# Pair 0's first element with a plain second product, block sums behind the last split, and x split first at the turn to stage two

## The reference

```python
def _L0(x, adj, S, W1, W2, W3):          # called with S = adj, so the weighting is adj * adj
    def _slconv(x, adj, S, W):
        return einsum('nm,bmh->bnh', adj * S, einsum('bnf,fh->bnh', x, W))
    h = relu(_slconv(x, adj, S, W1))     # 128 -> 256 features
    h = relu(_slconv(h, adj, S, W2))     # 256 -> 512
    return _slconv(h, adj, S, W3)        # 512 -> 128
def _L1(x, adj, Wg0, bg0, Wg1, bg1, Wih, Whh, bih, bhh):
    h = relu(einsum('ts,bsh->bth', adj, x @ Wg0 + bg0))
    h = relu(einsum('ts,bsh->bth', adj, h @ Wg1 + bg1))
    ...                                  # LSTMs over windows of p = 1..4 nodes
    return h
x = _layernorm(x + _L0(x, adj, adj, W1, W2, W3))
x = _layernorm(x + _L1(x, adj, ...))
```

## Time and profile before

| | |
|---|---|
| median of 3 runs | 1001.5 us (1000.24 to 1001.92) |
| the profiled execution | 1000.72 us |
| its span in the trace | 998.5 us |
| PE busy in the span | 970.3 us, 97% |
| DVE, ACT, POOL busy | 660.7, 434.8, 58.4 us |
| mean granted clock of PE | 0.99 |

### The profile page before, as it was taken

How to read it: one execution, slowest core, us unless ns; L and a number is a source line. 1 busy time by engine, 2 the same in 40 slices (tenths; PEclk the granted TensorE clock), 3 DMA queues, 4 the chain that set the end, 5 groups by cost and what they waited for, 6 DMA issues and landing times.

```text
span 998.5 us, 14421 instructions
## 1 busy us (share of the span) xinstructions
PE 970.3 (97%) x5267; PEld 846.1 (85%) x5267; DVE 660.7 (66%) x1447; ACT 434.8 (44%) x796; POOL 58.4 (6%) x46
## 2 busy tenths in 40 slices
PE   9789999999999999999989999999999999999994
PEld 7568898888988899888978889898988989898894
DVE  7865456654465554755396556877677786777987
ACT  6533323244133330343334444545454454554765
POOL 2600010002000020000000000101010010100000
PEclk9899999999999999999999999999999999999998
DMA  8000010200102001012700000000000000000001
GB/s 301 0 1 1 1 43 1 85 1 1 43 0 84 0 3 40 21 64 96 273 1 1 1 1 1 1 1 22 2 1 22 0 21 0 21 2 21 1 1 63
DMA packets 11287, 30.99 MB, mean 31 GB/s; under 512 B 1121, under 2 KB 2401, under 8 KB 11233
## 3 DMA queue, kind: packets, MB, share of 16 engines
q1 hardware_dynamic: 11232, 30.30, 8.3%
HBM read 22.95 MB, written 7.34 MB: 30 GB/s over the span
## 4 chain that ended last, share of the span: by engine, by line
PE 87%; DVE 8%; ACT 2%; issue 2%; DMA 1%; SPq 0%; DVEq 0%; ACTq 0%
PE ps L1201 23%; PE ps L866 20%; PE ps L842 10%; PE ps L843 10%; PE ps L844 10%; PE ps L1042 8%; PE ps L1254 2%; PE ps L1274 2%; DVE adj L1677 1%; DVE tile_sum L2096 1%; PE ps L1034 1%; DVE sx L1677 1%; PE ps L1316 1%; DVE stats L1694 1%; DMA xb<-in_x 1%
## 5 line engine op out<-in xcount | busy, mean ns | idle before, releaser
L866 PE MATMUL ps<-adj,t 128*128 128x512 f32 x528 | 124.9, 390 | 3.3 <-DVE y_raw L1868 1.5
L866 PEld LDWEIGHTS ps<-adj,t 128*128 128x128 f32 x528 | 98.1, 188 | 24.1 <-DVE y_raw L1868 2.0
L1042 PE MATMUL ps<-s,adj 128*128 128x256 f32 x768 | 94.0, 284 | 0.0
L866 PE MATMUL ps<-sx,t 128*128 128x512 f32 x396 | 92.1, 390 | 1.2 <-DVE sx L1677 0.8
L1042 PEld LDWEIGHTS ps<-s,adj 128*128 128x128 f32 x768 | 92.6, 192 | 0.0
L866 PEld LDWEIGHTS ps<-sx,t 128*128 128x128 f32 x396 | 74.2, 188 | 17.4 <-DVE sx L1677 1.2
L842 PE MATMUL ps<-adj,node 128*128 128x512 f32 x216 | 85.0, 394 | 2.5 <-DVE adj L1677 2.4
L844 PE MATMUL ps<-adj,node 128*128 128x512 f32 x216 | 84.8, 392 | 0.0
L843 PE MATMUL ps<-adj,node 128*128 128x512 f32 x216 | 84.6, 392 | 0.0
L1615 ACT ACTIVATE gates_x<-ps,lb 128x258 f32<-128x258 f32 (+1 forms) x156 | 66.5, 508 | 40.3 <-PE ps L1201 40.1
L1615 ACT ACTIVATE gates<-ps,lb 128x512 f32<-128x512 f32 (+2 forms) x117 | 66.7, 647 | 37.9 <-PE ps L1201 28.7
(11 more groups left out here) (244 smaller groups left out, 1806.8 us busy)
## 6 DMA issues: line engine op xcount, KB each, us to landing
xb<-in_x SPq DMA_DIRECT2D x7, 1024.0 KB, 4.8
sx_raw<-in_adj_t SPq DMA_DIRECT2D x8, 512.0 KB, 8.2
adj_raw<-in_adj_t SPq DMA_DIRECT2D x8, 512.0 KB, 7.2
out<-xb SPq DMA_DIRECT2D x7, 512.0 KB, 2.6
xn<-xb SPq DMA_DIRECT2D x3, 1024.0 KB, 4.0
xb<-xn SPq DMA_DIRECT2D x6, 512.0 KB, 6.6
xb<-in_x SPq DMA_DIRECT2D x2, 512.0 KB, 5.3
lw_raw<-in_wih_t SPq DMA_DIRECT2D x1, 1024.0 KB, 11.4
```

The lines of the kernel that those rows point to most:

```text
L866: last = pe.matmul(dst, t7[:, B_BLOCK[v], a, tile], A_BLOCK[v](b, t), start=start and t == 0 and (a, b) == (HI, HI), stop=t == QUARTER - 1 ...
L1042: last = pe.matmul(dst, adj[:, a, m, nt:nt + P], s3[:, b, m, :, :].rearrange("p j c -> p (j c)"), start=(m == 0 and t == 0 and (a, b) == ( ...
```

## The change

Three edits.

1. The second adjacency product of element 0 of pair 0 is done plainly: eight blocks, 96 matmuls, on the parts of the adjacency matrix itself and of the relu of the W1 product, whose high and low parts are now taken straight from PSUM ("0 h1 0" to "0 h1 3"; the low part in two instructions each). The T sums, the block sums' waits and the additions on DVE go away for this element.
2. The block sums on POOL begin when the low part of the last tile ("adj7") is there. A21 - A11 moves from DVE to POOL (four instructions more there, 16 in all). The splits of W2 and W3, of S1, S2, S3 and S4 move to later places: W2, W3 and S1 behind "0 h1 3", S2 behind the four C blocks, S3 and S4 among the h2 blocks.
3. In the last pair ACT takes "n x" and the high parts of tiles 0 and 1 of the new adjacency matrix before "from a11".

```diff
+        PLAIN = ["0 C11", "0 C12", "0 C21", "0 C22"]
-        MM_FIRST = ["x0 0", "x0 1", "x1 0", "x1 1"] + w1_names(0, 0, 4) + seven(0, FIRST_ORDER) + MM_TAIL
+        MM_FIRST = ["x0 0", "x0 1", "x1 0", "x1 1"] + w1_names(0, 0, 4) + PLAIN + MM_TAIL
+        X_H1 = ["x C12", "x C22", "0 h1 0", "0 h1 1", "x C11", "x C21", "0 h1 2", "0 h1 3", "w2 w3", "S1"] + PLAIN
-        HI_FIRST = (PRE + ["x C12", "x C22", "S1", "0 raw 0", "0 raw 1", "0 B11", "0 T1", "x C11", "x C21", "0 raw 2",
-                           "0 raw 3", "0 B21", "0 T2", "S2", "0 p1", "0 B22", "S4", "0 T3", "S3", "0 T4"]
-                    + hi_second(0, *C_FIRST) + HI_TAIL)
+        HI_FIRST = (PRE + X_H1 + ["S2"] + h2_names(0, 0, 0, K3) + ["S3"] + h2_names(0, 1, 0, 2) + ["S4"]
+                    + h2_names(0, 1, 2, K3) + HI_TAIL)
-        HI_LAST = HI_START + hi_second(0, *C_ORDER) + HI_ONE + FROM_A11 + ["n x"]
+        HI_LAST = HI_START + hi_second(0, *C_ORDER) + HI_ONE + ["n x"] + FROM_A11
-        LO_FIRST = (PRE + ["S3 sum", "x C12", "x C22", "0 T1 sum", "0 B11", "S1", "0 T2 sum", "0 T1", "x C11", "x C21",
-                           "0 T4 sum", "0 B21", "0 T2", "S2", "0 q", "0 T3 sum", "0 B22", "S4", "0 T3", "S3", "0 T4",
-                           "0 C11", "0 r"] + lo_second(0, *LO_C_FIRST) + LO_TAIL)
+        LO_FIRST = (PRE + X_H1 + ["S2"] + h2_names(0, 0, 0, K3) + ["S3"] + h2_names(0, 1, 0, 2) + ["0 s3t 0", "S4"]
+                    + h2_names(0, 1, 2, K3) + LO_TAIL)
...
+            pool.wait_ge(a_lo, prepared("adj7"))
             for t in range(QUARTER):
-                pool.wait_ge(*((sq_act, 5), (sq_done, 5), (sq_act, 6), (sq_done, 6))[t])
-                if t == 0:
-                    pool.wait_ge(sq_done, 1)
                 nc.gpsimd.tensor_tensor(sx_raw[:, S1, LO, t, :], a21(t), a22(t), ALU.add).then_inc(block_sum, 1)
...
+            for t in range(QUARTER):
+                nc.gpsimd.tensor_tensor(s3_diff[:, t, :], a21(t), a11(t), ALU.subtract).then_inc(block_sum, 1)
...
+                def plain_part(k, rows, half):
+                    of, dst = ((B11, T3), (B21, B22))[rows][k], bank("0 " + (("a", "e"), ("b", "c"))[k][half])
+                    for t in range(QUARTER):
+                        lo_done(f"0 h1 {2 * rows + t // 2}")
+                        last = product(dst, lambda i: t7[:, of, i, t * P:(t + 1) * P],
+                                       lambda i: adj[:, i, rows * QUARTER + t, half * BANK:(half + 1) * BANK],
+                                       (rows, t) == (0, 0), (rows, t) == (1, QUARTER - 1))
+                    return last
+                def plain_adjacency():
+                    for k in range(K2):
+                        if k == 1:
+                            lo_done("x C11", "x C21")
+                        for half in range(HALVES):
+                            plain_part(k, 0, half)
+                    for half in range(HALVES):
+                        for k in range(K2):
+                            signals(plain_part(k, 1, half), f"0 C{half + 1}{k + 1}")
...
                 def adj_block_lo(name):
...
-                    if name != "S4":
-                        dve.wait_ge(block_sum, {"S1": 2, "S2": 3}[name] * QUARTER)
+                    dve.wait_ge(block_sum, {"S1": 2, "S2": 4, "S4": 4}[name] * QUARTER)
...
                 if first:
-                    counted("S3 sum")
-                    nc.vector.tensor_tensor(s3_diff[:], sx_raw[:, S2, HI, :, :], sx_raw[:, S4, HI, :, :],
-                                            ALU.subtract).then_inc(a_lo, 1)
...
+                if last_pair:
+                    act.wait_ge(xb_in, 16 * (B - 2))
+                    hi_of("n x", node[:, HI, :], xb[:, 0].rearrange("p t c -> p (t c)"), ACT.Copy)
+                    tile_hi(0)
+                    tile_hi(1)
                 for u in range(2):
                     mm_done("a3 first")
                     hi_of(f"from a11 {u}", from_a11[:, u, :], bank(f"a3 {u}"), ACT.Copy)
-                if last_pair:
-                    act.wait_ge(xb_in, 16 * (B - 2))
-                    hi_of("n x", node[:, HI, :], xb[:, 0].rearrange("p t c -> p (t c)"), ACT.Copy)
```

More of the change, by code:

```diff
@@ L223, in build @@
         PRE = ["adj0 left", "x0 first", "adj0 right", "x1 first", "x0 rest", "adj1 left", "adj1 right",
-               "adj2 left", "adj2 right", "x1 rest", "adj3 left", "adj3 right", "adj4", "adj5", "adj6", "w1", "adj7",
-               "w2 w3"]
+               "adj2 left", "adj2 right", "x1 rest", "adj3 left", "adj3 right", "adj4", "adj5", "adj6", "w1", "adj7"]
         X_FIRST, HALVED = 2, 4
@@ L234, in h2_names, with seven @@
             return [f"{e} h2 {half} {g}" for g in range(g0, g1)]
-        ORDER, FIRST_ORDER = (1, 5, 6, 3, 7, 2, 4), (1, 5, 2, 6, 3, 7, 4)
-        def seven(e, order=ORDER):
-            return [f"{e} P{v}" for v in order]
+        ORDER = (1, 5, 6, 3, 7, 2, 4)
+        def seven(e):
+            return [f"{e} P{v}" for v in ORDER]
         def w1_names(e, u0, u1):
@@ L259, in hi_second @@
             return c_names(e, *names) + h2_names(e, 0, 0, K3) + h2_names(e, 1, 0, K3)
-        C_ORDER, C_FIRST = ("C12", "C22", "C11", "C21"), ("C11", "C12", "C22", "C21")
+        C_ORDER = ("C12", "C22", "C11", "C21")
+        X_H1 = ["x C12", "x C22", "0 h1 0", "0 h1 1", "x C11", "x C21", "0 h1 2", "0 h1 3", "w2 w3", "S1"] + PLAIN
         HI_ONE = (["1 raw 0", "1 raw 1", "1 B11", "1 T1", "1 raw 2", "1 raw 3", "1 T2", "1 B22", "1 p1", "1 T4",
@@ L273, in build @@
         HI_NEXT = HI_START + hi_second(0, *C_ORDER) + HI_TAIL
-        HI_LAST = HI_START + hi_second(0, *C_ORDER) + HI_ONE + FROM_A11 + ["n x"]
-        LO_C, LO_C_FIRST = ("C12 sum", "C12", "C22 sum", "C22", "C11", "C21 sum", "C21"), ("C12 sum", "C12", "C22 sum", "C22", "C21 sum", "C21")
+        HI_LAST = HI_START + hi_second(0, *C_ORDER) + HI_ONE + ["n x"] + FROM_A11
+        LO_C = ("C12 sum", "C12", "C22 sum", "C22", "C11", "C21 sum", "C21")
         def lo_second(e, *names):
@@ L374, in c_block, with h1_part @@
             return y2_raw[:, n[0], cols] if part == "raw" else y2[:, part, n[0], cols]
+        PLAIN_AT = {"C11": "a", "C12": "b", "C21": "e", "C22": "c"}
+        def h1_part(of, part, u, t=None):
+            one, other = ((B11, T3), (B21, B22))[u // 2]
+            tiles = [[P, 2]] if t is None else []
+            return bass.AP(tensor=of, offset=(2 * one + part) * BANK + (u % 2 * 2 + (t or 0)) * P,
+                           ap=[[7 * 2 * BANK, P], *tiles, [2 * (other - one) * BANK, 2], [1, P]])
         LW = 2 * SKIPS - 1
@@ L1069, in pair_products @@
                     w1_product(0, 3)
-                adjacency(0)
+                if first:
+                    plain_adjacency()
+                else:
+                    adjacency(0)
                 for g in range(K3):
@@ L1436, in raw @@
                     mm_done(f"{e} w1 {u}")
[L1437 to L1440, removed]
+                    hi_of(f"{e} raw {u}", h1_part(t7_raw, LO, u), bank(f"{e} w1 {u}").rearrange("p (t k c) -> p t k c", t=2, k=2), ACT.Relu)
                 def block_hi(e, name):
@@ L1457, in c_hi @@
                 def c_hi(e, name):
-                    if name == "C11":
+                    if first and e == 0:
+                        mm_done(f"0 {name}")
+                        hi_of(f"0 {name}", c_block(0, name, HI), bank("0 " + PLAIN_AT[name]), ACT.Copy)
+                    elif name == "C11":
                         mm_done(f"{e} P2")
@@ L1583, in _ @@
             pair(PAIRS - 1)
[L1586 to L1592, removed]
-                nc.scalar.activation(adj[:, HI, m, :], adj_raw[:, m, :], ACT.Copy).then_inc(b_hi, 1)
+            for m in range(2, MT):
+                tile_hi(m)
             act.wait_ge(acc_step, ADDED - 1)
@@ L1982, in outputs @@
                     c_lo(e, "C22")
-                    if not (first and e == 0):
-                        c_lo(e, "C11")
+                    c_lo(e, "C11")
                     c_sum(e, "C21")
@@ L1990, in outputs @@
                     h2_lo(e, 1, 2, K3)
-                outputs(0)
+                if not first:
+                    outputs(0)
                 t1_sum(1)
```

137 lines of the change are left out of this document (71 added, 66 removed).

## The result

The changed kernel takes 983.31 us (median of 4 runs, 983.24 to 983.72), the kernel before 1001.71 us (4 runs, 1000.24 to 1002.81): ratio 0.9818, 95% interval 0.9801 to 0.9835. That is 18.4 us less; 16.7 us was forecast, 984.8 us, and the range was 983.2 to 989.3, so the measured time lies at its lower end. The span of the profiled execution went from 998.5 to 981.7 us, 16.8 us less.

What follows compares the result with a forecast made beforehand. PE, busy 970.3 of 998.5 us, was taken to set the time. Gains of 11.6 us in the opening and 5.1 at the turn, 16.7 together, gave 984.0 against the profiled execution, 984.8 as median; range 983.2 to 989.3.

Steps and rivals of the forecast that it cites:

- The opening: From tile 7 to the first h2 matmul: PE's waits and low clock go, h2 at 54.98 not 66.77; 11.6 us gained.
- Tile 7's split: In the opening on DVE: ready at about 24.3, over 3 us before PE wants it at 27.60.
- the chain over ACT and DVE to "0 h1 0": In the opening behind the W1 product: PE to 31.2, ACT to 31.8, DVE to about 32.6; needed at 33.18.
- the 12 matmuls more: In element 0's plain product: 12 more matmuls of 0.227 us each cost PE 2.7 us.
- the low part in two halves: DVE's h1 low parts from PSUM, two half-width instructions: between 0.64 and 1.28 us, taken as 0.8.
- S2's split: On DVE before the h2 splits: ends at 60.0, must start by 60.3; slack 2.6 us before s3 wants h2.
- The turn: At the start of stage two: three waits and the low clock go, 5.2 us, of which 5.1 us was taken.
- DVE's queue of 16 instructions: Before the tile sum's low part at the turn: takes 18.4 us, its late start was the bound; now has 22.4 us.
- The rival with the low clock missing at the turn: Low clock not in every run before, so the turn gives 3.7 us and not 5.2: 986.3 us; chance 7%.
- A seam in the opening: PE waits 1 us or more at tile 7, W1 or first h1, then low clock: about 987.5 us; chance 12%.
- POOL holding up reads of PSUM: In the opening DVE's PSUM reads wait up to 1.27 us each, plain product's third tile 4.4 us late: 989.2; chance 4%.
- a smaller gain at the turn: DVE gets ahead less than reckoned at stage two's start: 987.8 us, or 989.9 if the edit does nothing; chance 14%.

Runs made afterwards that it cites:

- e2: The changed kernel without its edit at the turn in the last pair (ACT's order there as before): 988.81 us, ratio 0.9884 to the kernel before.
- e5: The kernel before with only POOL's late block sums and A21 - A11 on POOL, seven products kept: 1002.17 us, ratio 1.0017 to the kernel before.
- e3: The changed kernel with POOL's block sums begun as early as in the kernel before, plain product kept: 987.24 us, 3.9 us over the changed kernel.
- e6: The changed kernel with 12 sums more on POOL (A21 - A11 made four times): 988.19 us, 4.9 us over the changed kernel.
- e4: The changed kernel with "n x" still first, but the high parts of tiles 0 and 1 behind "from a11" again: 983.89 us.
- e9: The kernel before with ten matmuls that nobody reads, put on PE before the wait for the tile sum's low part: 999.27 us, ratio 0.9989.
- e1: The kernel before with only the edit at the turn ("n x" and tiles 0 and 1 ahead of "from a11"): 996.06 us, ratio 0.9956.
- e7: The kernel before, unchanged, profiled a second time: 1000.76 us.
- e11: The kernel before, unchanged, profiled a fourth time: 1000.86 us.
- e10: The kernel before, unchanged, profiled a third time: 1000.77 us.
- e8: The changed kernel with A21 - A11 back on DVE as one instruction behind tile 7's split, 12 sums on POOL: 983.60 us.

## Why the prediction was right

**The opening, 11.6 us.** Right step by step. The profile has 66.77 - 55.05 = 11.7, and e2 12.0 by medians. The queues and waits came out as forecast; how much of the gain is the plain form's own is open (e5). Tile 7's split was there in time because POOL had not begun (e3), the chain over ACT and DVE to "0 h1 0" fitted into W1's matmuls, and the 12 matmuls more cost 2.7 us of PE with no other price. The one term that I had only bounds for, the low part in two halves, came out at 1.48 us for two blocks, 0.74 a block against the 0.8 taken. POOL's end, forecast at about 49, was 48.1. S2's split ended at 60.0 as forecast, and e6 confirms both the slack and what lies behind it.

**The turn, 5.1 us.** Right: 11.09 - 5.92 = 5.17 us in the profile. DVE's queue of 16 instructions (18.4 us) was the bound; in the changed kernel it begins at 477.45, 22.5 us before PE takes the row sums at 499.93, and e4 shows the 4 us of spare time in it. 3.7 us of the gain is waiting; the other part is the low clock, and e9 shows that as a thing of its own, at 1.33 us in the same stretch.

**The sum.** 16.7 forecast; 16.8 between the two spans. The 18.4 between the medians is 1.6 more, and no step of mine has it; it brought the time to the lower end of the range. Three parts of it can be named. The other runs of the changed kernel are 0.4 under its profiled one. The median of before in the first comparison, 1001.71 us from four runs, is 1.0 above its profiled execution. And the profiled executions differ by 17.0 us, 0.2 more than their spans. Later the median of before was 1000.78, 1001.17 and 1001.02, against which the changed kernel gains 17.5 to 17.9. So most of the excess is scatter, and what sets that stays open. The rival with the low clock missing at the turn (7%) did not occur in a profile: it was there in all four, in e2, and in e5, where it began only within the fifth or sixth of the eight row sum matmuls and reached into the product behind (0.70 in 517.2 to 520.5).

**The rivals.** A seam in the opening, POOL holding up reads of PSUM, and a smaller gain at the turn did not occur. In the changed kernel two PSUM splits take 1.38 us in the middle of POOL's sums, and four of POOL's sums beside them 5.06: no exclusion, as the Trainium skill's "GPSIMD Engine Reference", "Key points", has it, which names only instructions in a two-port mode or with two SBUF inputs.

## What to carry to other kernels

Where the engine that sets the time waits for another, look at what stands ahead of the awaited instruction in its queue, and what runs beside it; a short form that needs prepared data (seven products) can lose, in the first round, to the long form that needs none, until the preparation is hidden (it did so here in the orders that were run). Try the halves of such a change separately before you drop one: late sums alone lost 1 to 2 us here, and with the plain form they are worth 3.9. Price a wait of PE with the lower clock behind it, where nothing else holds the next step: at the turn 2.45 us of waiting cost 1.3 to 1.5 us more, but in the opening of the kernel before the lower clock on W1 only shortened the wait behind it (e1).

## What the runs showed of the hardware that was not expected

**A late load moves the whole opening of the kernel before.** In the six profiles with that opening the first h2 matmul comes 58.9 us after ACT's first split of x of element 1, which waits for the load of x. The rest of ACT's opening stands behind it in its queue.

| profile | ACT's split of x | first h2 matmul | between |
|---|---|---|---|
| before | 7.83 | 66.77 | 58.94 |
| e7 | 7.97 | 66.89 | 58.92 |
| e11 | 8.06 | 66.97 | 58.91 |
| e10 | 8.15 | 67.09 | 58.94 |
| e1 | 8.36 | 67.29 | 58.93 |
| e9 | 8.49 | 67.44 | 58.95 |

The changed kernel doesn't follow it: in e4 the split is at 8.19 and h2 at 54.75, in the changed kernel 7.92 and 55.05. There PE has no pause from tile 7 to h2, so PE is the bound and not the queue of ACT and DVE.

**The place of the lower clock.** In the opening it fell on tile 7 and part of W1 in all four profiles of the kernel before, but almost wholly on W1 in e1 and e9, whose opening has the same instructions: tile 7 at 1.00, W1 at 0.50. By the table this made no difference to h2. e1 and e9 are one profile each, and also the two in which tile 7 starts latest (30.18 and 30.30, against 29.65 to 29.96), so whether the edit 480 us later, the load or chance puts it there isn't shown. "TensorE: Matmul & The Clock Gate" of the Trainium skill, "What's actually happening", says that the look at PE's activity isn't tied to the kernel; these profiles agree in that the moment at which the clock falls differs, by 1 us among the four of one kernel (30.1 to 31.1) and by 5 to 6 us to e1 and e9 (36.0 and 36.1).

**Scatter.** The runs of the kernel before differ by up to 3.7 us (999.08 to 1002.81), and those of e5, which waits in both places too, by 2.63. Those of the kernels with waits of one place alone differ by 0.27 (e2), 0.35 (e1), 0.62 (e3), 0.89 (e9) and 1.14 (e6), those of the changed kernel by 0.48, of e4 by 0.30 and of e8 by 0.60. The load of x moved the opening by 0.66 us among the profiles; that is a part of it, and no profile shows the rest.
